# The out projection of the second token half cut into 384 + 128 columns, and its first piece issued ahead of the last value products

## What is computed

```python
h = shift_token(x)                       # half of the features come from the token before
q, k, v = split(h @ wqkv)                # 8 heads of 64
q, k = l2norm(q) * qs, l2norm(k) * ksc   # then rotary_xpos(q, k)
o = local_attention(q, k, v)             # window of 128 tokens and the window before it
x = x + o @ wo                           # wo is 512 x 256: the out projection
h = layer_norm(shift_token(x)) * lg + lb
a, g = split(h @ w1 + b1)
x = x + (a * gelu(g)) @ w2 + b2
```

## Time and profile before

| what | value |
|---|---|
| median of 3 runs | 2295.97 us (2294.08 to 2304.67) |
| profiled execution, its own time | 2298.97 us |
| its span, first to last instruction | 2296.1 us |
| PE busy | 87% of the span |
| DVE, ACT, POOL busy | 63%, 54%, 35% |
| mean granted TensorE clock | 0.96 of full speed |
| part `layers` in the span | from about 890 us on, 8 iterations of about 175 us |

### The profile page before, as it was taken

How to read it: one execution, slowest core, us unless ns; L and a number is a source line. 1 busy time by engine, 2 the same in 40 slices (tenths; PEclk the granted TensorE clock), 3 DMA queues, 4 the chain that set the end, 5 groups by cost and what they waited for, 6 DMA issues and landing times.

```text
span 2296.1 us, 36136 instructions
## 1 busy us (share of the span) xinstructions
PE 1990.5 (87%) x11968; PEld 1241.2 (54%) x11968; DVE 1457.9 (63%) x3942; ACT 1243.2 (54%) x2980; POOL 798.9 (35%) x663
## 2 busy tenths in 40 slices
PE   5566899999988746999999999989899999999998
PEld 3232233333322424667667667667667667667666
DVE  5457788888885435746756755746755755756754
ACT  1110666666667323754754764763754764764663
POOL 2223321122232335505505605614613613623620
PEclk9896899999999877999999999999999999999999
DMA  4645855554540552000000000011200000000000
GB/s 144 152 124 114 147 128 83 84 73 71 105 123 11 147 156 78 1 24 14 1 24 15 1 19 19 2 68 43 73 19 19 20 19 19 19 19 19 20 1 28
DMA packets 124455, 128.97 MB, mean 56 GB/s; under 512 B 50460, under 2 KB 101232, under 8 KB 123248
## 3 DMA queue, kind: packets, MB, share of 16 engines
q1 hardware_dynamic: 123696, 117.75, 22.2%
q0 software_dynamic: 576, 8.91, 1.0%
HBM read 75.51 MB, written 50.86 MB: 55 GB/s over the span
## 4 chain that ended last, share of the span: by engine, by line
PE 38%; DVE 10%; ACT 8%; issue 5%; POOL 2%; DMA 0%; DVEq 0%; SPq 0%; ACTq 0%; POOLq 0%
PE qkv_ps L1338 5%; PE s_ps L1439 4%; DVE rot_s L1886 4%; PE s_ps L1384 4%; PE pt_ps L1518 3%; PE o_ps L1518 3%; PE pt_ps L1452 3%; PE o_ps L1477 3%; ACT p_sb L1630 3%; DVE p_sb L1895 3%; PE s_ps L1397 2%; PE qkv_ps L1397 2%; PE pt_ps L1439 2%; PE o_ps L1439 2%; POOL inv_norm L1780 2%
## 5 line engine op out<-in xcount | busy, mean ns | idle before, releaser
L717 ACT ACTIVATE probs<-st_ps 128x512 f32<-128x512 f32 (+3 forms) x768 | 329.8, 494 | 166.7 <-PE st_ps L625 166.2
L1338 PE MATMUL qkv_ps<-w_qkv,x_parts 128*128 128x512 f32 x1152 | 308.6, 411 | 32.7 <-DVE x_parts L1860 23.6
L1630 ACT ACTIVATE p_sb<-p_sb,negmax 128x256 f32<-128x256 f32 (+1 forms) x512 | 249.2, 489 | 63.2 <-DVE negmax L1895 63.1
L610 PE MATMUL s_ps<-k_stack,q_stack 96*128 96x512 bf16 (+3 forms) x768 | 242.1, 346 | 41.3 <-DVE piece_negmax L762 25.7
L762 DVE CUSTOM_DVE_ANT_0 seen<-s_ps,causal 128x128 f32<-128x128 f32 (+3 forms) x512 | 233.6, 484 | 43.7 <-PE s_ps L610 43.5
L1338 PEld LDWEIGHTS qkv_ps<-w_qkv,x_parts 128*128 128x128 f32 x1152 | 211.9, 194 | 80.0 <-issue 38.5
L625 PE MATMUL st_ps<-q_stack,k_stack 98*128 98x512 bf16 (+3 forms) x768 | 240.8, 334 | 14.4 <-ACT probs L717 10.1
L1895 DVE CUSTOM_DVE_ANT_0 p_sb<-s_ps,band 128x256 f32<-128x256 f32 (+1 forms) x512 | 185.4, 401 | 89.3 <-PE s_ps L1384 85.5
L844 POOL TENSOR_SCALAR_AFFINE_SELECT probs<-probs 128x512 f32<-128x512 f32 x128 | 81.6, 637 | 415.4 <-ACT probs L717 415.4
L1788 POOL TENSOR_TENSOR rot_c<-qn,turn_by 128x512 f32<-128x512 f32 x128 | 178.6, 1415 | 130.8 <-PE turn_ps L1364 105.0
L1646 ACT COPY p_t<-pt_ps 128x512 f32<-128x512 f32 (+1 forms) x256 | 143.2, 559 | 127.6 <-PE pt_ps L1452 126.3
(11 more groups left out here) (146 smaller groups left out, 3487.5 us busy)
## 6 DMA issues: line engine op xcount, KB each, us to landing
qk_scratch<-parts SPq DMA_DIRECT2D x64, 192.0 KB, 2.8
q_stack<-qk_scratch SPq DMA_DIRECT2D x96, 128.0 KB, 6.7
k_stack<-qk_scratch SPq DMA_DIRECT2D x96, 128.0 KB, 7.1
w_ffn<-ffn_weights POOLq DMA_DIRECT2D x4, 2176.0 KB, 11.4
v_scratch<-v_out SPq DMA_DIRECT2D x32, 256.0 KB, 2.6
v_sb<-v_scratch SPq DMA_DIRECT2D x16, 512.0 KB, 10.3
x_in<-xt_scratch SPq DMA_DIRECT2D x16, 512.0 KB, 4.1
ffn_weights<-w_high SPq DMA_DIRECT2D x2, 2176.0 KB, 8.1
```

The costliest lines, as they stand in the source:

```text
L610: pe.matmul(s_ps[i % 3][:, 0:kw], q_stack[0:STK, slot, h, qt * P:(qt + 1) * P], k_stack[0:STK, slot, h, k0:k0 + kw], start=True, stop=True ...
L717: act.activation(probs[:, n % 3, h, q0:CH], st_ps[i % 3][:, q0:CH], ACT.Exp).then_inc(exp_done.sem, 1)
L1338: mm = pe.matmul(qkv_ps[:, part * CH:(part + 1) * CH], x_parts[:, w % XR, xp, k, :], w_qkv[:, wp, k, part * INNER:(part + 1) * INNER], sta ...
L1630: act.activation(p_sb[:, u % 4, h, k0:PW], p_sb[:, u % 4, h, k0:PW], ACT.Exp, scale=-1.0, bias=negmax[:, u % 4, h:h + 1], accum_out=total[ ...
```

## The change

The second half's 512 columns are now two runs (`OUT_RUNS`): tokens 512 to 895 (384 columns, windows 4 to 6) and tokens 896 to 1023 (128 columns, window 7). `project_out`, `residual` and `out_bank` take a run number r (0: first half as before). Run 1 goes to the same score banks, 384 columns wide; run 2 puts both output tiles side by side in the values' bank `v_ps`. Run 1, tile 0 is issued on PE at u = 33, after the last `turn_probs` and before the last `spread_sums` and `values`; run 1, tile 1 and both tiles of run 2 stand at the head of `feed_forward`. Run 1 waits for `o_scaled` of window 6, run 2 for that of window 7. On DVE the residual of run 1, tile 0 stands before `split_norm(it, 0)`, and the three others behind it. Semaphore counts go from 4 to 6 per iteration.

```diff
+OUT_RUNS = ((0, CH), (CH, T - P), (T - P, T))
+RUNS = len(OUT_RUNS)
...
-        out_bank = lambda c, m: ln_ps[m] if c == 0 else s_ps[m]
+        out_bank = lambda r, m: (ln_ps[m], s_ps[m][:, 0:CH - P], v_ps[:, m * P:(m + 1) * P])[r]
...
-            def project_out(it, c, m):
-                if c == 0 and m == 0:
+            def project_out(it, r, m):
+                t0, t1 = OUT_RUNS[r]
+                if r == 0 and m == 0:
                     pe.wait_ge(ffn_go.sem, ffn_go.of(it, 0))
                     pe.wait_ge(qn_ready.sem, qn_ready.of(it, NT - 1))
-                if c == 1 and m == 0:
+                if r == 1 and m == 0:
                     pe.wait_ge(s_masked.sem, s_masked.of(it, 2 * UNITS - 1))
-                pe.wait_ge(o_scaled.sem, o_scaled.of(it, (c + 1) * WPC - 1))
+                if r == 2 and m == 0:
+                    pe.wait_ge(v_copied.sem, v_copied.of(it, NT - 1))
+                pe.wait_ge(o_scaled.sem, o_scaled.of(it, t1 // P - 1))
                 for k in range(INNER // P):
-                    mm = pe.matmul(out_bank(c, m)[:, :], w_out[:, k, m * P:(m + 1) * P],
-                                   o_t[:, k, :], start=k == 0, stop=k == INNER // P - 1)
+                    mm = pe.matmul(out_bank(r, m), w_out[:, k, m * P:(m + 1) * P],
+                                   o_t[:, k, t0 % CH:t0 % CH + t1 - t0], start=k == 0, stop=k == INNER // P - 1)
                 mm.then_inc(wo_ready.sem, 1)
...
             def tokens_first(it, c):
-                pe.wait_ge(mid_ready.sem, mid_ready.of(it, (c + 1) * KD - 1))
+                pe.wait_ge(mid_ready.sem, mid_ready.of(it, (RUNS if c else 1) * KD - 1))
...
+                    if u == UNITS + 1:
+                        project_out(it, 1, 0)
                     if u >= 4 and u % 2 == 0:
                         values((u - 4) // 2)
...
-                project_out(it, 1, 0)
                 project_out(it, 1, 1)
+                project_out(it, 2, 0)
+                project_out(it, 2, 1)
                 up(it, 0, 0)
                 tokens_first(it, 1)
...
-            def residual(it, c, m):
-                dve.wait_ge(wo_ready.sem, wo_ready.of(it, c * KD + m))
...
+            def residual(it, r, m):
+                t0, t1 = OUT_RUNS[r]
+                dve.wait_ge(wo_ready.sem, wo_ready.of(it, r * KD + (m if r < RUNS - 1 else KD - 1)))
...
-                s = slice(m + c * CH, m + (c + 1) * CH)
-                dve.tensor_tensor(x_mid[:, m, s], out_bank(c, m)[:, :], x_in[:, m, s], ALU.add).then_inc(mid_ready.sem, 1)
+                s = slice(m + t0, m + t1)
+                dve.tensor_tensor(x_mid[:, m, s], out_bank(r, m), x_in[:, m, s], ALU.add).then_inc(mid_ready.sem, 1)
...
+                residual(it, 1, 0)
                 split_norm(it, 0)
...
-                residual(it, 1, 0)
                 residual(it, 1, 1)
+                residual(it, 2, 0)
+                residual(it, 2, 1)
                 for j in range(HT):
```

More of the change, by code:

```diff
@@ L1188, in layers @@
         o_copied = count("o_copied2", NT, 1)
-        wo_ready = count("wo_ready", NC * KD, 4)
-        mid_ready = count("mid_ready2", NC * KD, 4)
+        wo_ready = count("wo_ready", RUNS * KD, 4)
+        mid_ready = count("mid_ready2", RUNS * KD, 4)
         ln_ready = count("ln_ready", NC * 2)
@@ L1291, in _ @@
                         load_tables()
-                    sp.wait_ge(mid_ready.sem, mid_ready.of(it, NC * KD - 1))
+                    sp.wait_ge(mid_ready.sem, mid_ready.of(it, RUNS * KD - 1))
                     load_x(it + 1)
@@ L1426, in up @@
                 elif i == 1:
-                    pe.wait_ge(mid_ready.sem, mid_ready.of(it, NC * KD - 1))
+                    pe.wait_ge(mid_ready.sem, mid_ready.of(it, RUNS * KD - 1))
                 elif i == HT:
@@ L1897, in mask_scores @@
                                              negmax[:, u % 4, h:h + 1]).then_inc(s_masked.sem, 1)
-            def residual(it, c, m):
-                dve.wait_ge(wo_ready.sem, wo_ready.of(it, c * KD + m))
-                if c == 0 and m == 0 and it <= B:
+            def residual(it, r, m):
+                t0, t1 = OUT_RUNS[r]
+                dve.wait_ge(wo_ready.sem, wo_ready.of(it, r * KD + (m if r < RUNS - 1 else KD - 1)))
+                if r == 0 and m == 0 and it <= B:
                     for stored in out_stored:
                         dve.wait_ge(stored, it * (16 * NC) + 16)
-                s = slice(m + c * CH, m + (c + 1) * CH)
-                dve.tensor_tensor(x_mid[:, m, s], out_bank(c, m)[:, :], x_in[:, m, s], ALU.add).then_inc(mid_ready.sem, 1)
+                s = slice(m + t0, m + t1)
+                dve.tensor_tensor(x_mid[:, m, s], out_bank(r, m), x_in[:, m, s], ALU.add).then_inc(mid_ready.sem, 1)
             tile = lambda t: ln_ps[t % TC // 2][:, (t % 2) * D:(t % 2 + 1) * D]
```

## The result

The changed kernel takes 2275.52 us (median of 4 runs, 2272.28 to 2281.70), beside 2297.76 for the kernel before (4 runs): a ratio of 0.9893, 95% interval 0.9875 to 0.9910. Forecast were 2273.2 and a range of 2267 to 2286. The profiled execution of the changed kernel took 2281.70 us, its span 2280.0 us. All medians in this document are of ordinary executions; one execution of e1 (5745 us) and one of e4 (2952 us) took far longer and are left out.

What follows compares the result with a forecast made beforehand. PE, busy 87%, was taken as the bound, idle at the seam; 3.02 us less a 0.17 switch gave 2.85, times 8 22.8, from 2298.97 to 2276.2, less 3.0 for the median: 2273.2 us, range 2267 to 2286.

Steps and rivals of the forecast that it cites:

- The gaps and what fills them: PE between attention and feed forward: idle of 1.43 and 1.78 us, less a 0.17 switch, filled with out-projection passes.
- The price of the passes: Out projection on PE: a 384-column pass takes 0.322 us, a 128-column pass 0.109 us.
- The rival with visible weight loads: 128-column out-projection passes: loads show, 0.19 to 0.217 us per pass, time about 2285 us; chance 0.12.
- The added wait: Turning of the last sums and last value products on PE: 1.15 us later than before, behind the early piece.
- The near tie: Before the first up projection: the split allows loading at 1001.11, PE's own work at 1001.19, 0.08 us apart.
- the prediction's sign: Before the first up projection: the second split should end within 0.2 us of the first up load.
- The hidden residual: DVE between last scaling and second split: residual of run 1, tile 0 takes about 0.56 us and costs nothing.
- The handover: Change to the up projection on PE: one 0.17 us switch that short passes may not cover, taken off 3.02 us.
- The median of the runs is 3.0 below that execution: Whole time: 3.0 us taken off 2276.2, the profiled execution less the gain, to forecast the median.
- 8 times one gain: All eight iterations: each saves the same 2.85 us, 22.8 us in all.
- The clock rival: Narrow passes at the seam bring the 1.2 GHz level, 2.7 us per stretch; two stretches give 2316 us; chance 0.04.
- Given back later: PE's waits for masked scores at the start of attention swallow the gain; time about 2295 us; chance 0.05.

Runs made afterwards that it cites:

- e1: Changed kernel with the cut kept, but the first 384-column piece issued behind the last value products and its residual behind the split; 2284.11 us.
- e4: Changed kernel with both 384-column pieces issued ahead of the turning of the last sums; 2294.02 us.
- e2: Changed kernel with the residual of run 1, tile 1 also put ahead of the split on DVE; 2279.46 us.
- e3: Changed kernel with the second half cut into 256 + 256 columns instead of 384 + 128, order unchanged; 2270.67 us.
- e6: Changed kernel with scale_norm ahead of the last copy_output on ACT and split_norm ahead of the last scale_output on DVE; 2273.59 us.

## Why the prediction was right

- **The gaps and what fills them.** Forecast was a seam (from the last loads of unit 31's turning to the first up pass) of about 8.7 us in place of 11.63. Measured: from 1001.10 + 0.42 to 1010.12 plus the 0.09 by which the first up group is longer than the others, 8.69, a gain of 2.94 on the 11.63 from 992.68 to 1004.31, where the first up pass stood by the same reckoning (1003.91 + 1.96 - 1.56). e1 and e4 show that each gap needs its own piece.
- **The price of the passes.** 384 columns: (2.75 - 0.486) / 7 = 0.323 us (0.322 forecast), with 0.486 for one pass's duration. 128 columns: (1.95 - 0.275) / 15 = 0.112 (0.109). The rival with visible weight loads wanted 0.19 to 0.217.
- **The added wait.** The last value products start 3.61 us behind the loads of unit 31's turning (1001.10 to 1004.71), before 2.44: 1.17 later (1.15 forecast). All that hangs on them moved by the same 1.17: the second split ended 8.75 us behind that point, before 7.58.
- **The near tie.** The split ended at 1009.85 and the up projection loaded at 1010.09; the least distance is 0.12, so 0.12 us of room were left, against a forecast of 0.08. (The split ended 0.24 us ahead of the load; the prediction's sign was 0.2.) e2 used it up and lost the rest, e3 and e6 widened it and won nothing.
- **The hidden residual.** 0.55 us on DVE (0.56 forecast) between scaling and split, with 0.12 to spare: free.
- **The handover.** I took 0.17 off for a switch behind the narrow passes. Of that at most 0.07 came: without it the sum gives a seam of 8.62 us (1001.30 - 992.68), and 8.69 were measured. The steady gain is 2.92 us per ordinary period (175.31 to 172.40 and the one before), 2.85 were forecast.
- **What was mis-sized.** Two terms, both small; their errors cancel in part. "The median of the runs is 3.0 below that execution": the three runs I had put the median at 2295.97; with 4 to 14 runs it is 2297.67 to 2300.96, so that execution (2298.97) was an ordinary one. This put the forecast too low. And the gain was larger than 22.8: the profiles give 24.9 (the medians differ by 22 to 25 us), which put it too high. That 2273.2 lies only 2.3 us from the measured 2275.52 is in part luck, as single runs spread over 10.
- **The clock in iteration 3.** "8 times one gain" left it out. The period of iterations 3 to 4 fell by 4.1 us, 1.1 more than the others. Behind PE's 3.47 us of idle for the second layer's weights the 1.2 GHz level came as before, but later and for half as long: in windows of 1 us it stands from about 1 us ahead of the down passes for 6.8 us before, and from within them for 3.4 now.

```profile
1547.00 5.31 PE L1525 MATMUL pt_ps<-hidden,w_ffn 128*128 128x512 f32 x15 [3.47 <-DVE hidden L2002]
1552.64 0.95 PE L1525 MATMUL pt_ps<-hidden,w_ffn 42*128 42x512 f32 x3 [0.34 <-DVE hidden L2002]
```

  The 18 down passes took from 1547.00 to the next group's start at 1553.52, 6.52 us, where 7.30 were needed before, with a mean granted clock of 0.74 against 0.59. e1 shows what that time is without any low clock:

```profile
1544.96 3.76 PE L1523 MATMUL pt_ps<-hidden,w_ffn 128*128 128x512 f32 x15 [3.47 <-DVE hidden L2000]
1550.60 0.96 PE L1523 MATMUL pt_ps<-hidden,w_ffn 42*128 42x512 f32 x3 [1.88 <-DVE hidden L2000]
1544.96:1551.49 6.53, 4.65 (x18) 3.22 (x18) 6.53 (x12) 3.41 (x5) 0.00 (x0) 1.00 0.00 0
```

  At full clock the first 15 passes are done early, PE waits 1.88 us for the last slice of `hidden` from DVE, and the whole takes the same 6.53. So DVE sets this time, and the low clock cost 0.8 us in the kernel before and nothing in the changed one. That is 0.8 of the 1.1; the rest was not followed up. It also means that the rival on the clock priced its stretch wrongly: 7.36 less 4.64, the 2.7 us, is mostly DVE's wait and not the clock's.
- **The clock rival.** Over the seam the clock was 1.00, as forecast, and so it was in all eight seams of the changed kernel. The second row is the stretch of iteration 3:

```profile
1001.52:1010.24 8.72, 8.72 (x56) 6.21 (x54) 2.93 (x5) 5.48 (x8) 0.00 (x0) 1.00 0.01 2
1547.00:1553.50 6.50, 6.17 (x18) 4.35 (x18) 6.50 (x12) 3.40 (x5) 0.00 (x0) 0.74 0.00 0
```

- **Given back later** did not happen: the waits in the rest of the iteration are those of before (for masked scores 30.0 us, 29.9 before; for `q_t` 15.7, 15.5 before).

## What to carry to other kernels

Where the engine that sets the time waits twice in a chain of small steps, split a block of work by what it depends on and put the part that is ready into the first gap and the rest into the second. Size the early part by the gap: what exceeds it delays everything behind (e4: two pieces put early gave back 18 of 22 us), and if the other engines' chain hangs on the delayed step, work out when that chain ends before moving anything. Measure such a change by the period between two fixed instructions in the profile; here the last period repeats within 0.1 us (172.40 and 172.38, 171.55 and 171.48) where whole times spread over 10. Look at the granted clock of such a period before comparing it.

## What was not expected of the hardware

- The parts ahead of the layers differ between executions by up to 13 us (the first `up(0, 0)` at 996.60 to 1010.12 in the profiles of this study), with the same instructions; in the stretch from 200 to 400 us the granted clock was 0.90 on the mean in the profile of the kernel before and 0.87 in that of the changed one. The cause of that spread was not tested.
- The wait of 0.3 us that e2 made is not named as idle anywhere, since a narrow pass's modelled duration (0.275 us) is longer than the distance to the next one (0.111). For short passes only the distance of starts tells.
- A wait of PE is not enough to tell whether the clock falls. In iteration 3 of e1 PE waited 3.47 us and the clock stayed at 1.00; in the same place of the kernel before it fell to 0.59 on the mean, and in its first period it fell behind a wait of 2.03 us.
